# Moving the wait for the last scatters of a mixture-of-experts kernel from GpSimd to SyncE

## The reference

```
logits = x @ gate_w ; scores = softmax(logits) ; topk_w, topk_idx = top_k(scores, 2)      # 8 experts
g = silu(x @ w_gate[e]) * (x @ w_up[e])                                                    # 512 -> 352, per expert
routed = sum over the token's two experts of  topk_w * (g @ w_down[e])                     # 352 -> 512
shared = silu(x @ sw_gate) * (x @ sw_up) @ sw_down                                         # 512 -> 704 -> 512
out = x2 + gb * (routed + shared)
```

## Time and profile before

| | us |
|---|---|
| median of three runs (715.85, 719.1, 719.9) | 719.1 |
| the profiled execution | 717.99 |
| its span | 716.2 |
| TensorE busy | 682.1 (95% of the span) |
| VectorE busy | 469.6 |
| GpSimd busy | 169.4 |

### The profile page before, as it was taken

The page is one execution under the profiler, slowest core; times in us unless marked ns, Lnnn a source line. Parts: engine busy times, 40 slices in busy tenths (PEclk is TensorE's granted clock), DMA queues, the critical chain, the costliest instruction groups (busy, mean ns, idle before and its releaser), DMA issues.

```text
span 716.2 us, 10569 instructions
## 1 busy us (share of the span) xinstructions
PE 682.1 (95%) x3796; PEld 562.6 (79%) x3796; DVE 469.6 (66%) x967; ACT 258.0 (36%) x478; POOL 169.4 (24%) x221
## 2 busy tenths in 40 slices
PE   5899999999979999999999999999999999999992
PEld 1477677777857887887887887989898998989891
DVE  1987769836899886467767835665574847556451
ACT  1555344535344342412013024435362534436130
POOL 1232223310012110000000032334435353540403
PEclk9799999999999999999999999999999999999997
DMA  8923131104135624230320533657665575852505
GB/s 275 361 84 104 38 83 30 41 4 162 59 133 177 213 89 135 86 106 13 103 96 1 165 107 118 192 120 191 103 198 73 187 131 148 193 97 59 67 0 67
DMA packets 44219, 82.52 MB, mean 115 GB/s; under 512 B 7529, under 2 KB 15721, under 8 KB 43634
## 3 DMA queue, kind: packets, MB, share of 16 engines
q1 hardware_dynamic: 35730, 62.06, 26.8%
q0 software_dynamic: 8448, 19.93, 14.6%
HBM read 59.93 MB, written 23.22 MB: 116 GB/s over the span
## 4 chain that ended last, share of the span: by engine, by line
PE 63%; DVE 8%; issue 2%; ACT 1%; POOL 1%; POOLq 0%; DVEq 0%
PE bank L1560 19%; PE bank L1562 19%; PE bank L1561 19%; PE bank L1811 2%; PE bank L1791 1%; DVE rows L1183 1%; DVE u L1173 1%; DVE m L1147 1%; DVE st L989 1%; DVE hx L1195 1%; DVE mw L1152 1%; POOL out_rows L613 1%; PE bank L1869 1%; PE bank L1770 0%; PE bank L1882 0%
## 5 line engine op out<-in xcount | busy, mean ns | idle before, releaser
L1560 PE MATMUL bank<-ht,ew 128*128 128x288 f32 (+1 forms) x384 | 114.6, 299 | 0.2 <-DVE ht L1458 0.2
L1561 PE MATMUL bank<-ht,ew 128*128 128x288 f32 (+1 forms) x384 | 113.1, 294 | 0.0
L1562 PE MATMUL bank<-ht,ew 128*128 128x288 f32 (+1 forms) x384 | 112.8, 294 | 0.0
L613 POOL DMA_INDIRECT out_rows<-y,si x40 | 61.9, 1547 | 110.7 <-DVE y L1489 100.0
L1560 PE MATMUL bank<-xt,sgu 128*128 128x512 f32 x176 | 69.5, 395 | 0.4 <-DVE rows L1183 0.4
L1560 PEld LDWEIGHTS bank<-ht,ew 128*128 128x128 f32 (+1 forms) x384 | 68.7, 179 | 1.3 <-issue 0.6
L1561 PEld LDWEIGHTS bank<-ht,ew 128*128 128x128 f32 (+1 forms) x384 | 69.0, 180 | 0.3
L1562 PEld LDWEIGHTS bank<-ht,ew 128*128 128x128 f32 (+1 forms) x384 | 68.7, 179 | 0.0
L1561 PE MATMUL bank<-xt,sgu 128*128 128x512 f32 x176 | 68.7, 390 | 0.0
L1562 PE MATMUL bank<-xt,sgu 128*128 128x512 f32 x176 | 68.6, 390 | 0.0
L1560 PE MATMUL bank<-wkv,xt 128*128 128x512 f32 x128 | 55.2, 431 | 2.8 <-DVE xt L1018 2.8
(11 more groups left out here) (302 smaller groups left out, 1512.1 us busy)
## 6 DMA issues: line engine op xcount, KB each, us to landing
xring<-in_L_attn_X SPq DMA_DIRECT2D x32, 256.0 KB, 2.8
ewst<-in_L_ffn_w_gate SPq DMA_DIRECT2D x8, 704.0 KB, 5.3
ewst<-in_L_ffn_w_up SPq DMA_DIRECT2D x8, 704.0 KB, 4.3
slots<-in_L_wmod SPq DMA_DIRECT2D x4, 1024.0 KB, 6.1
x_d<-rows SPq DMA_DIRECT2D x16, 256.0 KB, 2.0
h_d<-hx SPq DMA_DIRECT2D x16, 256.0 KB, 2.0
xrow<-x_d SPq DMA_DIRECT2D x16, 256.0 KB, 2.8
out_rows<-xrow SPq DMA_DIRECT2D x16, 256.0 KB, 2.2
```

The lines of the kernel that those rows point to most:

```text
L613: pool.indirect_dma_start(out=out, out_offset=bass.IndirectOffsetOnAxis(ap=si[0:CR[j], par, j:j + 1], axis=0), in_=y[0:CR[j], j, :], in_of ...
L1560: nc.tensor.matmul(dst, a[0], b[0], start=first, stop=False)
L1561: nc.tensor.matmul(dst, a[0], b[1], start=False, stop=False)
L1562: return nc.tensor.matmul(dst, a[1], b[0], start=False, stop=last)
```

## The change

The function `scatter` gets a third argument. For the last entry GpSimd leaves out the wait on `y_out` and the increment of `added`, and comes to the end of its program. SyncE, behind its loop of weight loads, reads `final` into a register, waits for the full count of `y_out`, and comes to the end of its own.

```diff
             with sp.Fori(0, more) as i:
                 for par in range(2):
                     load_expert(2 * i + par + 2, par)
+            final = nc.sync.value_load(loops[0:1, 1:2], min_val=E - 2, max_val=ENTRIES - 2)
+            sp.wait_ge(y_out, 16 * CT * (final + 2))
+            sp.nop(nofuse=True)
...
-            def scatter(u, par):
+            def scatter(u, par, last=False):
...
-                pool.wait_ge(y_out, 16 * CT * (u + 1))
-                pool.nop(nofuse=True).then_inc(added, 1)
+                if not last:
+                    pool.wait_ge(y_out, 16 * CT * (u + 1))
+                    pool.nop(nofuse=True).then_inc(added, 1)
...
             for par in range(2):
-                scatter(final + par, par)
+                scatter(final + par, par, par == 1)
```

## The result

| | before | changed |
|---|---|---|
| median, first comparison (4 runs each) | 719.14 | 714.61 |
| ratio, 95% interval | | 0.9946 (0.9922 to 0.9969) |
| median, repeated later (17 and 12 runs) | 717.55 | 715.17 |
| ratio, 95% interval | | 0.9968 (0.9951 to 0.9984) |
| profiled execution / its span | 717.99 / 716.2 | 713.40 / 711.6 |

The forecast of 3.3 us, a ratio of 0.9954, lies in both intervals. Nothing that varies ahead of it enters it.

A forecast was written before the change was run, and what follows sets the result against it. GpSimd's tail was taken as the bound: last scatter's issue, landing, then a 6.6 us DRAIN. Starting the DRAIN's work 3.3 us earlier gave 717.99 - 3.3 = 714.7 profiled, 719.1 - 3.3 = 715.8 us by the median; range 712.6 to 720.1.

The forecast's parts named there:

- The forecast of 3.3 us: End of the program: GpSimd's DRAIN work starts at 706.08 instead of 709.38, saving 3.3 us; chance 0.50.
- GpSimd alone ends the program, and the last piece of its tail is a DRAIN of 6.6 us: Program's end: the last 12.3 us are GpSimd's alone: issue, landing, then a DRAIN of 6.6 us.
- The 6.6 us are work owed for the DMAs, not a wait: GpSimd's final DRAIN: its 6.6 us are work GpSimd owes for 80 indirect DMAs, all landed.
- one DRAIN with no DMA behind it: GpSimd's DRAIN ahead of all gathers and scatters: ends 0.05 us behind the last iota, so costs 0.05 us.
- The work begins with the end of the last issue and runs beside the landing: 3.3 us: GpSimd's final DRAIN: starts its work at 706.08, ends at 712.7; gain 3.3 us.
- The rival that waits for the landings first: Final DRAIN: waits for landings, then does its 6.6 us; time 719.0, no change; chance 0.30 together with a timer.
- A timer from the last issue: Final DRAIN: the 6.6 us are a timer ending at 716 anyway; no change; chance 0.30 together with landings first.
- The pass that is made twice: Final DRAIN: its 6.6 us pass repeats if something hasn't landed; 3.3 us slower, 722.4; chance 0.10 (slower).
- More overlap with the issue: Final DRAIN: work done beside the last scatter's issue; gain 4.7 us, time 714.4; chance 0.10 for all more-overlap cases.
- the DRAIN shorter without the pause: Final DRAIN: far shorter, so SyncE's wait is the end; gain 6.6 us, 712.5; within more overlap's 0.10.
- SyncE's added load and wait are free: SyncE's end: load takes 0.7 us, 59 us before the landing; SyncE finishes 3.3 us ahead of GpSimd's DRAIN.
- The record of the DRAIN: Sign in the changed profile: GpSimd's final DRAIN starts near 704.7, ends near 712.7, a record of some 8.0 us.

The follow-up runs named there:

- the second DRAIN: Kernel before with one more GpSimd DRAIN behind its last wait, directly ahead of the block's own; 718.98 us in a single run.
- the early ones: Changed kernel with a GpSimd DRAIN added before the last two entries' scatters (711.43 us, ratio 0.9904) or between them (711.94 us, 0.9923).
- with 30 owed: Changed kernel with a GpSimd DRAIN added at the head of every pass of its loop; 713.42 us against 719.45 for the kernel before.
- with the last one in flight: Changed kernel, but GpSimd waits for the last entry's first four scatters and SyncE alone for the fifth; tail 11.4 us.
- 20 copies of 16 bytes: Changed kernel with 20 more 16-byte DMAs issued by GpSimd behind the first gathers and waited for at once; 718.09 us against 719.45.

## Why the prediction was right, and what it had wrong

- *GpSimd alone ends the program, and the last piece of its tail is a DRAIN of 6.6 us.* Right: without it the tail is 5.8 to 6.0 us, and the kernel before is faster by 6.6 us.
- *The 6.6 us are work owed for the DMAs, not a wait.* Right for the kernel before, where all has landed: 82 ns for each of 80, and 0.04 us for a DRAIN with nothing owed. I had argued it from one DRAIN with no DMA behind it, which couldn't tell a fixed cost from one by number; the second DRAIN and the early ones did.
- *The work begins with the end of the last issue and runs beside the landing: 3.3 us.* The size is right (12.38 - 9.14 = 3.24 us by the tails), the mechanism is half right. Only the first half of the work can run beside the landing; the second waits for it. Here half the work is 80 x 0.041 = 3.28 us and the last landing is 3.35 us behind the last issue, so the half just fills the gap, and the sum came out as if all of it could overlap. That the two are nearly equal is luck. With fewer DMAs owed, or a later landing, the second half is paid behind the landing and my picture is too short: with 30 owed it gives a tail of 5.8 to 6.0 us, and the run showed 7.3.
- *The rival that waits for the landings first* was therefore no mere rival: its half is real. It was priced for all 6.6 us, and gave no gain. A timer from the last issue is out: the DRAIN ended 9.9 us behind the last issue before and 6.7 us behind it now.
- *The pass that is made twice* doesn't happen: with the last one in flight the DRAIN took 6603 ns, and with 80 owed and the last in flight it ended as the rule gives. More overlap with the issue doesn't either, nor is the DRAIN shorter without the pause: the record starts early, but it ends 6.67 us behind the end of the issue.
- *SyncE's added load and wait are free*: right, a ratio of 0.9995 for them alone, and in the changed kernel its DRAIN is over 3.2 us before GpSimd's ends.
- *The record of the DRAIN*: 8.0 us from the start of the last scatter's instruction was forecast; it was 8.37, as the record starts 0.28 us ahead of that instruction and ends 6.67 us behind the issue in place of 6.60. The forecast set aside what the Trainium skill says ("VectorE: DVE Perf Modes", section "The DRAIN you can't avoid"), some 12 ns on all five engines. The page says it of the runtime's boilerplate DRAINs. The DRAIN at line 75 is left out by an argument of the kernel's own block, so the rule need not be about it. Its figure is met there by SyncE's DRAIN (13 ns) and by none of the others (722 to 6603 ns).

## What to carry to other kernels

Where GpSimd issues DMAs, look at its DRAIN at the end of the program: count the DMAs issued since its last DRAIN and expect 82 ns for each, as measured here from 5 to 100 of them. If the DRAIN stands behind the last landing, it is cheaper to put an early DRAIN where GpSimd is idle and everything has landed (6.0 us here) than to hand the final wait to another engine (3.2 us here). The early one takes both halves of the work out of the end; handing over the wait hides only the half that can run beside the landing. And when a forecast is a few tenths of a per cent, read a distance inside the profile that excludes the work ahead: the tails repeated to 0.1 us (9.14 and 9.09), the medians' differences came out as 4.5 and 2.4.

## What the runs showed that I had not expected

- A DRAIN on GpSimd costs by the number of DMAs issued since the last one, not by their size or kind: 10 gathers, 10 scatters and 20 copies of 16 bytes fit one price of 2 x 41 ns.
- Its time comes out in two equal parts: one runs beside the last landing, the other only behind it.
- The debt doesn't carry over in any form that shows. In the two kernels without the DRAIN at the end, the first DRAIN of the profiled execution takes 169 and 171 ns, as in the others, and the scatters and gathers take as long as before. What ran on the core ahead of a profiled execution isn't in its trace.
